# A state-space, mixture and attention block on one core: ScalarE applies the three normalisations, VectorE keeps their statistics

## The chip, the cores and the metric

One core of a Trainium2 chip runs the whole program. The metric is the device time of one execution in microseconds, as a median of several runs. PE is TensorE, DVE is VectorE, ACT is ScalarE, POOL is GpSimd and SP is SyncE, whose queue issues the transfers.

## The reference

The input is 4096 tokens of width 256 (two sequences of 2048). Four layers follow each other, each with a residual and a layer norm without scale behind it:

```
x = layernorm(x + mamba(x))      # the mamba normalises x once more at its start (with ln_g, ln_b)
x = layernorm(x + moe(x))        # 4 experts, two of them weighed per token
x = layernorm(x + attention(x))  # 16 heads, keys and values with a cross product
x = layernorm(x + ffn(x))
layernorm(x) = (x - mean) / sqrt(var + 1e-5)      # over the 256 features of a token
mamba: h[t] = exp(delta*A) * h[t-1] + delta*B*x,  y[t] = sum over 16 states of h[t]*C[t]
```

## The kernel before

The program has two stages with a barrier between them. The first, `mamba_moe_qkv`, holds everything up to the queries, keys and values; the second is the attention and the last layer. Only the first is changed.

The first stage cuts the tokens into 8 chunks of 512. A chunk lies in SBUF as `[128, 4, 256]` while tokens are on the partitions (`xn_tok`, `x1_tok`, `x2_tok`), and as `[128, 2 or 4, 512]` once it is transposed. Each engine runs the same function `iteration(i)` for i = -1 to 9 (i = 3 to 5 in a hardware loop). One iteration works on four chunks at once: `i` is scanned (16 states, one in each of 16 slots n), `f = i+1` is projected and convolved, `m = i-1` goes through the output projection, the router and the experts, and `q = i-2` gets its second norm and its queries, keys and values. The order on an engine is written out by hand through `if n == ...` lines; engines are tied by semaphores and each takes its instructions strictly in that order.

In one slot ScalarE forms four decays (`decays`, L708) for the slot after, VectorE multiplies (L952) and scans (L963) in two halves and copies the last column of `h` into `state`, times a flag that is 0 where a sequence begins (`keep_state`, L970). GpSimd then multiplies `h` by C (`times_c`, L1181) and adds it to `y` (`add_y`, L1192). The scan of a slot waits for the sum of two slots before it, since `h` has two buffers.

There are three norms of a chunk in this stage. For each, VectorE forms mean and variance of a token (`norm_stats`, L97 and L101) in the middle of a slot, GpSimd turns the variance into `r = (var + eps) ** -0.5` with two small operations (`scale`, L1249 and L1252), and VectorE applies the norm at the end of that slot with four tensor_scalar operations (`norm_apply`, L110), one for each 128 tokens:

```python
last = nc.vector.tensor_scalar(dst[:, i, :], src[:, i, :], mv[:, i, 0:1], r[:, i:i + 1],
                               ALU.subtract, ALU.mult)
```

- Norm 2, of chunk q, is applied in slot 1. `turn_x2` (PE, L572) transposes its result, behind `project_out` (L479) of chunk m; ScalarE copies it (L802), PE projects v (L563) and then z of chunk i (`project_z`, L449).
- Norm 1, of chunk m, is applied in slot 2. Its input needs `project_out` (the residual sum is L982). `turn_x1` (PE, L488) transposes its result in slot 3.
- Norm 0, of chunk i+2, is applied in slot 12 and transposed in slot 3 of the next iteration (`turn_xn`, L426).

ScalarE's order in slots 1 to 3 is: four decays, `y_begin` (L716); four decays, `copy_v` (L802, L805), `gates` (L722, the silu of z); four decays, `copy_qk` (L810 first: v by tokens, which frees a PSUM bank for the projection of q), `copy_x1` (L775), `copy_xn` (L728). In slot 4 it writes `xb` (L739), for which VectorE's `conv` (L912) waits. In slot 5 ScalarE's `routers` (L779) waits for VectorE's `crossed` (L1074, L1076), since both use `hid`. In slot 12 it copies B and C (`copy_bc`, L751), then four decays, then the copies of delta (L760).

Of the kernel before, what the change touches and what calls it, by code (L numbers as in the profile page):

```python
# [36 lines left out]
NORM_STEPS = 3  # L37
# [91 lines left out]
def mamba_moe_qkv(nc, a, scr, chunks=NCH):  # L129


    with ExitStack() as ctx:
# [28 lines left out]
        def col(name, i=0):  # L161
# [51 lines left out]
        powers = sb("powers", [P, 2, TT])  # L213
# [9 lines left out]
            q_stored k_stored kb_stored neg_ready powers_set ln0_scaled ln1_scaled ln2_scaled passed_sp passed_pe passed_dve passed_pool""".split()  # L223
# [71 lines left out]
        def _(sp):  # L295
# [31 lines left out]
            def store_x2(c):  # L327
                tok = bass.ds(c * CH, CH)
                sp.wait_ge(s["ln2_steps"], (c + 1) * NORM_STEPS)
                sp.dma_start(scr["x2"][tok, :].rearrange("(s p) n -> p s n", p=P), x2_tok[:])\  # L330
                    .then_inc(s["x2_stored"], 16)
# [77 lines left out]
        def _(pe):  # L409
# [10 lines left out]
            def turn_xn(c):  # L420
                pe.wait_ge(s["ln0_steps"], (c + 1) * NORM_STEPS)
# [61 lines left out]
            def turn_x1(c):  # L483
                pe.wait_ge(s["ln1_steps"], (c + 1) * NORM_STEPS)
# [82 lines left out]
            def turn_x2(c):  # L567
                pe.wait_ge(s["ln2_steps"], (c + 1) * NORM_STEPS)
# [131 lines left out]
        def _(act):  # L700
# [71 lines left out]

            def copy_x1(c):
# [58 lines left out]
            def iteration(i):  # L832
# [3 lines left out]
                for n in range(NS):  # L836
# [50 lines left out]
            act.wait_ge(s["setup_dve"], 5)  # L887
            iterations(act, iteration)
# [3 lines left out]
        def _(dve):  # L892
# [5 lines left out]

            def norm0_apply(c):
                dve.wait_ge(s["ln0_scaled"], 2 * c + 2)  # L900
                norm_apply(nc, s["ln0_steps"], xn_tok[:], xn_tok[:], ln_tmp)
# [76 lines left out]
            def norm1_stats(c):  # L978
                at_least(dve, s["ln2_steps"], c * NORM_STEPS)
# [7 lines left out]

            def norm1_apply(c):
                dve.wait_ge(s["ln1_scaled"], 2 * c + 2)
                norm_apply(nc, s["ln1_steps"], x1_tok[:], x1_tok[:], ln_tmp)  # L990
# [69 lines left out]

            def norm2_apply(c):
                dve.wait_ge(s["ln2_scaled"], 2 * c + 2)
                at_least(dve, s["x2_stored"], 16 * c)
                if not isinstance(c, int) or c > 0:
                    for k in range(KD):
                        wait_full(dve, c - 1, ("x2T", k))
                norm_apply(nc, s["ln2_steps"], x1_tok[:], x2_tok[:], ln_tmp)
# [32 lines left out]
            def iteration(i):  # L1100
# [3 lines left out]
                for n in range(NS):  # L1104
# [46 lines left out]
                    if n == 12 and inside(i + 2):  # L1151
                        norm0_apply(i + 2)
# [9 lines left out]
            v.memset(powers[:, 1], -0.5).then_inc(s["powers_set"], 1)  # L1162
            dve.wait_ge(s["w_mamba"], W_MAMBA)
# [6 lines left out]
            norm0_apply(0)  # L1170
# [4 lines left out]
        def _(pool):  # L1175
# [748 lines left out]
```

## Time and profile before

| | us |
|---|---|
| median of 3 runs (lowest, highest) | 4110.46 (4109.77, 4111.14) |
| the profiled execution, its own time | 4113.52 |
| its span, first to last instruction | 4111.7 |
| the first stage in it, up to the barrier | about 2172 |
| VectorE, TensorE, ScalarE, GpSimd busy over the span | 2964.8, 3500.6, 2195.3, 1515.1 |

Line numbers (L110) are lines of the kernel before. In a timeline row the first number is the start, the second the time from the start to the end of the group, and xN the number of instructions that were merged in it. In brackets stands the idle time of the engine ahead of the row and what ended it. A mean of a group is in ns.

### The profile page before, as it was taken

The page shows a single profiled execution, that of the slowest core. Times are in us where ns is not written, and L with a number is a line of the kernel's source. Part 1 is how long each engine was busy: PE and PEld are TensorE (multiplying, and loading weights), DVE is VectorE, ACT ScalarE, POOL GpSimd, SP SyncE. Part 2 cuts the span into 40 slices and gives each one's busy share as a digit, 9 for nine tenths or more (in the row PEclk, how much of TensorE's full clock was granted, in tenths as well). Part 3 has the DMA queues.
Part 4 walks back from the last instruction along what each step waited for, and adds up shares of the span by engine and source line. Part 5 has one row for each costly group of instructions (what it writes and reads, how often), then busy time and mean ns, then how long its engine had stood idle before and what let it go on. Part 6 is the DMA issues. An engine that isn't in the chain of part 4 may idle for free. (4 is left out here: it accounts for less than half of the span.)

```text
span 4111.7 us, 49896 instructions
## 1 busy us (share of the span) xinstructions
PE 3500.6 (85%) x14625; PEld 1599.7 (39%) x14625; DVE 2964.8 (72%) x3436; ACT 2195.3 (53%) x3556; POOL 1515.1 (37%) x1244
## 2 busy tenths in 40 slices
PE   4258888787878879788985999999999999999898
PEld 1025545354444545445540323222323232322565
DVE  4897786868778687685117878787878787878443
ACT  4344455545554454553210777777777777777221
POOL 2997686767777777687100000000000000000110
PEclk8579899899998989899995999999999999999999
DMA  2112112122121221212113000000000000000001
GB/s 95 31 37 65 61 53 77 54 70 78 57 75 44 80 69 60 70 59 98 49 36 99 17 18 17 18 21 21 18 18 17 18 17 18 22 20 29 15 31 36
DMA packets 110803, 183.45 MB, mean 45 GB/s; under 512 B 14495, under 2 KB 84599, under 8 KB 101817
## 3 DMA queue, kind: packets, MB, share of 16 engines
q1 hardware_dynamic: 110521, 180.09, 14.1%
q8 instruction: 128, 2.10, 0.2%
q14 instruction: 154, 1.26, 0.1%
HBM read 153.95 MB, written 26.09 MB: 44 GB/s over the span
## 5 line engine op out<-in xcount | busy, mean ns | idle before, releaser
L1688 DVE TENSOR_REDUCE tile_max<-ps 128x1 f32<-128x1024 f32 x1076 | 1268.1, 1220 | 287.5 <-PE ps L1479 284.9
L1633 ACT ACTIVATE probs<-ps 128x512 f32<-128x512 f32 x2056 | 1116.5, 598 | 492.4 <-PE ps L1493 467.2
L1181 POOL TENSOR_TENSOR h<-h,c_sb 128x512 f32<-128x512 f32 x512 | 678.7, 1356 | 421.9 <-DVE state L970 421.8
L1493 PE MATMUL ps<-qs,ks 101*128 101x512 bf16 x2056 | 712.8, 385 | 1.2
L1479 PE MATMUL ps<-ks,qs 99*128 99x512 bf16 x2152 | 668.8, 393 | 49.0 <-DMA ks<-scratch_kb 41.2
L963 DVE TENSOR_TENSOR_SCAN h<-decay,state,ps 128x512 f32<-128x512 f32 x512 | 627.5, 1267 | 58.5 <-POOL y_sum L1192 27.8
L1192 POOL TENSOR_TENSOR y_sum<-y_sum,h 128x512 f32<-128x512 f32 x512 | 641.3, 1284 | 8.5
L534 PE MATMUL ps<-x1T,e_w 128*128 128x512 f32 x1024 | 491.6, 629 | 103.0 <-ACT hid L779 102.6
L1503 PE MATMUL ps<-probs,vh 128*32 128x512 f32 x4096 | 551.5, 611 | 24.5 <-issue 24.5
L1805 POOL COPY vh<-v_all 128x256 f32 (+1 forms) x32 | 12.7, 402 | 1433.4 <-PE ps L1503 1368.1
L555 PE MATMUL ps<-e_w,hid 128*128 128x256 f32 x2048 | 454.2, 380 | 11.2 <-ACT hid L779 7.5
L1493 PEld LDWEIGHTS ps<-qs,ks 101*128 101x128 bf16 x2056 | 198.9, 97 | 644.2 <-ACT probs L1633 434.9
L779 ACT ACTIVATE hid<-ps,cols 128x512 f32<-128x512 f32 x288 | 193.2, 686 | 452.2 <-PE ps L534 423.7
L555 PEld LDWEIGHTS ps<-e_w,hid 128*128 128x128 f32 x2048 | 386.7, 190 | 82.2 <-issue 28.4
L708 ACT ACTIVATE decay<-delta,neg_a 128x512 f32<-128x512 f32 x512 | 335.0, 712 | 136.1 <-DVE h L963 129.7
L534 PEld LDWEIGHTS ps<-x1T,e_w 128*128 128x128 f32 x1024 | 202.4, 202 | 365.0 <-issue 225.7
L952 DVE TENSOR_TENSOR ps<-du,ps 128x1024 f32<-128x1024 f32 x256 | 312.5, 1221 | 6.5 <-PE ps L417 3.3
L1479 PEld LDWEIGHTS ps<-ks,qs 99*128 99x128 bf16 x2152 | 208.8, 99 | 274.3 <-issue 50.5
L1052 DVE SCALAR_TENSOR_TENSOR x_tok<-ps,cw,x_tok 128x256 f32<-128x256 f32 x128 | 55.2, 473 | 270.4 <-PE ps L555 270.4
L417 PE MATMUL ps<-bc,sel 96*128 96x512 bf16 x128 | 53.8, 421 | 169.6 <-DVE ps L952 169.6
L1503 PEld LDWEIGHTS ps<-probs,vh 128*32 128x32 f32 x4096 | 81.0, 108 | 220.6 <-ACT probs L1633 179.4
L479 PE MATMUL ps<-w_out,gate 128*128 128x256 f32 x256 | 76.7, 473 | 67.0 <-DVE x_tok L1052 62.7
(172 smaller groups left out, 3002.6 us busy)
## 6 DMA issues: line engine op xcount, KB each, us to landing
e_w<-in_e_w SPq DMA_DIRECT2D x64, 1024.0 KB, 7.0
c_sb<-scratch_c SPq DMA_DIRECT2D x128, 256.0 KB, 3.5
qs<-scratch_q SPq DMA_DIRECT2D x210, 64.0 KB
ks<-scratch_k SPq DMA_DIRECT2D x210, 64.0 KB
scratch_q<-parts SPq DMA_DIRECT2D x16, 384.0 KB, 4.0
scratch_k<-parts SPq DMA_DIRECT2D x16, 384.0 KB, 7.5
xr<-scratch_x SPq DMA_DIRECT2D x10, 512.0 KB, 4.0
xn_tok<-in_x SPq DMA_DIRECT2D x8, 512.0 KB, 4.9
```

Source lines behind the costliest of these rows:

```text
L534: last = mm(bank(key), e_w1[:, e % 2, k, i * P:(i + 1) * P], x1T[:, k, :], start=k == 0, stop=k == KD - 1)
L555: last = mm(ps[:, DOWN_BANK[at], i * D:(i + 1) * D], hid[:, k, (2 * pair + i) * P:(2 * pair + i + 1) * P], e_w2[:, e % 2, k, :], start=k = ...
L708: fn(decay[:, n % 2, m, :], delta[:, m, :], ACT.Exp, scale=neg_a[:, n * DB + m:n * DB + m + 1]).then_inc(s["decay_ready"], 1)
L952: v.tensor_tensor(ps[:, 0:2, :], du[:, 2 * half:2 * half + 2], ps[:, 2 + n % 2:3 + n % 2, :].to_broadcast([P, 2, CH]), ALU.mult)\
L963: v.tensor_tensor_scan(h[:, n % 2, m, :], decay[:, n % 2, m, :], ps[:, m % 2, :], state[:, n, m:m + 1], ALU.mult, ALU.add)\
L1181: last = nc.gpsimd.tensor_tensor(h[:, n % 2, m, :], h[:, n % 2, m, :], c_sb[:, n % C_RING, :], ALU.mult)
L1192: last = nc.gpsimd.tensor_tensor(y[:, m, :], y[:, m, :], h[:, n % 2, m, :], ALU.add)
L1479: last = mm(ps[:, slot(side) + i, :], qs[0:K_MAX, j, t * P:(t + 1) * P], ks[0:K_MAX, j, k * CH:(k + 1) * CH], start=True, stop=True)
L1493: mm(ps[:, S_BANK[i], :], ks[0:K_ALL, j, step * P:(step + 1) * P], qs[0:K_ALL, j, qc * CH:(qc + 1) * CH], start=True, stop=True).then_inc( ...
L1503: last = mm(ps[qc * VW:(qc + 1) * VW, AV_BANK, :], vh[:, j, step, :], probs[:, step % 2, qc, :], start=step == 0, stop=step == KT - 1)
L1633: fn(probs[:, step % 2, qc, :], ps[:, S_BANK[i], :], ACT.Exp)\
L1688: v.tensor_reduce(tile_max[:, t, half:half + 1], ps[:, slot(side):slot(side) + PAIR, :].rearrange("p a n -> p (a n)"), AX.X, ALU.max).then ...
```

## The change

ScalarE applies the norm with its own scale and bias, `x * r + (-mean * r)`. GpSimd forms the bias with two more small operations (four in all for each norm). VectorE keeps the statistics. Those who waited for the third step of the statistics semaphore (`turn_xn`, `turn_x1`, `turn_x2`, `store_x2`, `norm1_stats`) wait for a semaphore that ScalarE raises. Norm 2 stands on ScalarE in slot 1 behind `y_begin`, norm 1 in slot 2 behind `gates`, norm 0 in slot 12 behind `copy_bc`. Apart from this, `keep_state` takes the flag as a scalar operand of tensor_scalar where it was a second tensor.

```diff
-def norm_apply(nc, steps, src, dst, tmp):
-    mv, r = tmp[1], tmp[5]
+def norm_apply(nc, done, src, dst, tmp):
+    r, shift = tmp[5], tmp[6]
     for i in range(src.shape[1]):
-        last = nc.vector.tensor_scalar(dst[:, i, :], src[:, i, :], mv[:, i, 0:1], r[:, i:i + 1],
-                                       ALU.subtract, ALU.mult)
-    last.then_inc(steps, 1)
+        last = nc.scalar.activation(dst[:, i, :], src[:, i, :], ACT.Identity, scale=r[:, i:i + 1],
+                                    bias=shift[:, i:i + 1])
+    last.then_inc(done, 1)
...
+            def norm0(c):
+                act.wait_ge(s["ln0_scaled"], (c + 1) * SCALE_STEPS)
+                norm_apply(nc, s["ln0_done"], xn_tok[:], xn_tok[:], ln_tmp)
+            def norm1(c):
+                act.wait_ge(s["ln1_scaled"], (c + 1) * SCALE_STEPS)
+                norm_apply(nc, s["ln1_done"], x1_tok[:], x1_tok[:], ln_tmp)
+            def norm2(c):
+                act.wait_ge(s["ln2_scaled"], (c + 1) * SCALE_STEPS)
+                at_least(act, s["x2_stored"], 16 * c)
+                if not isinstance(c, int) or c > 0:
+                    for k in range(KD):
+                        wait_full(act, c - 1, ("x2T", k))
+                norm_apply(nc, s["ln2_done"], x1_tok[:], x2_tok[:], ln_tmp)
...
                     if n == 1 and inside(i):
                         y_begin(i)
+                    if n == 1 and inside(q):
+                        norm2(q)
                     if n == 2:
                         if inside(q):
                             copy_v(q)
                         if inside(i):
                             gates(i)
+                        if inside(m):
+                            norm1(m)
...
                     if n == 12 and inside(f):
                         copy_bc(f)
+                    if n == 12 and inside(i + 2):
+                        norm0(i + 2)
...
-                v.tensor_tensor(state[:, n, :], h[:, n % 2, :, CH - 1], keep.to_broadcast([P, DB]), ALU.mult)\
+                v.tensor_scalar(state[:, n, :], h[:, n % 2, :, CH - 1], keep, None, ALU.mult)\
...
-                    if n == 1 and inside(q):
-                        norm2_apply(q)
-                    if n == 2 and inside(m):
-                        norm1_apply(m)
-                    if n == 12 and inside(i + 2):
-                        norm0_apply(i + 2)
...
-                pool.wait_ge(s[name + "_steps"], c * NORM_STEPS + 2)
-                nc.gpsimd.tensor_tensor(ln_tmp[2], ln_tmp[1][:, :, 1], powers[:, 0], ALU.add)\
-                    .then_inc(s[name + "_scaled"], 1)
-                pool.wait_ge(s[name + "_scaled"], c * 2 + 1)
-                nc.gpsimd.tensor_tensor(ln_tmp[5], ln_tmp[2], powers[:, 1], ALU.pow)\
-                    .then_inc(s[name + "_scaled"], 1)
+                pool.wait_ge(s[name + "_steps"], (c + 1) * NORM_STEPS)
+                nc.gpsimd.tensor_tensor(ve, mv[:, :, 1], powers[:, 0], ALU.add).then_inc(scaled, 1)
+                nc.gpsimd.tensor_tensor(half, mv[:, :, 0], powers[:, 2], ALU.mult).then_inc(scaled, 1)
+                pool.wait_ge(scaled, at + 1)
+                nc.gpsimd.tensor_tensor(r, ve, powers[:, 1], ALU.pow).then_inc(scaled, 1)
+                pool.wait_ge(scaled, at + 3)
+                nc.gpsimd.tensor_tensor(shift, half, r, ALU.mult).then_inc(scaled, 1)
```

## Rows read from the trace of the kernel before

**Rows 1.** Window: length, busy of PE, PEld, DVE, ACT, POOL; clock; DMA share; GB/s

```profile
1100.00:1350.00 250.00, 205.03 (x641) 117.36 (x640) 192.16 (x217) 126.71 (x175) 184.42 (x151) 0.91 0.21 66
```

**Rows 2.** VectorE's groups of lines in the first stage: busy, mean | idle before

```profile
L970 DVE TENSOR_TENSOR state<-h,cols 128x4 f32<-128x4 f32 x128 | 60.9, 476 | 4.8 <-DVE h L963 0.2
L110 DVE TENSOR_SCALAR x_tok<-x_tok,ln_mv,ln_r 128x256 f32<-128x256 f32 x64 | 60.0, 997 | 4.8 <-POOL ln_r L1252 4.2 <-issue 0.5
...
L110 DVE TENSOR_SCALAR xn_tok<-xn_tok,ln_mv,ln_r 128x256 f32<-128x256 f32 x32 | 29.3, 976 | 2.9 <-POOL ln_r L1252 2.9
...
L1085 DVE TENSOR_SCALAR k_f<-k_f,temp 128x512 f32<-128x512 f32 x16 | 7.0, 479 | 0.0
```

**Rows 3.** VectorE's timeline in iteration 5 (1211 to 1465 us)

```profile
1240.59 4.99 DVE L110 TENSOR_SCALAR x_tok<-x_tok,ln_mv,ln_r 128x256 f32<-128x256 f32 x4 [0.19 <-issue]
...
1281.01 0.75 DVE L912 SCALAR_TENSOR_TENSOR xb<-ps,cols,xb 128x509 f32<-128x509 f32 x1 [3.06 <-ACT xb L739]
...
1289.38 2.94 DVE L1074 TENSOR_TENSOR soft<-soft,hid 48x512 f32<-48x512 f32 x2
```

**Rows 4.** TensorE's timeline in the same iteration, slots 1 to 3

```profile
1234.62 9.01 PE L479 MATMUL ps<-w_out,gate 128*128 128x256 f32 x32 [8.83 <-DVE x_tok L1052]
...
1245.64 1.09 PE L572 MATMUL ps<-ident,x_tok 128*128 128x128 f32 x8 [1.79 <-DVE x_tok L110]
...
1251.01 7.03 PE L449 MATMUL ps<-xnT,w_in 128*128 128x512 f32 x16
...
1263.08 10.10 PE L563 MATMUL ps<-x1T,wqkv 128*128 128x512 f32 x16 [3.95 <-ACT hid L810]
```

**Rows 5.** ScalarE's timeline in the same iteration

```profile
1258.69 1.28 ACT L708 ACT_TABLE_LOAD   x1
1259.98 2.56 ACT L708 ACTIVATE decay<-delta,neg_a 128x512 f32<-128x512 f32 x4
1262.45 1.06 ACT L810 ACTIVATE hid<-ps 128x512 f32<-128x512 f32 x2
...
1432.16 0.69 ACT L760 ACTIVATE pre<-ps,cols 128x512 f32<-128x512 f32 x1 [7.59 <-PE ps L466]
```

**Rows 6.** Who waited for VectorE's L110, and for L1076

```profile
  PE ps L572: 12.8, 7
...
  ACT hid L779: 3.8, 3
...
  ACT L779: 3.7, 3
```

**Rows 7.** ScalarE's groups of lines in the first stage

```profile
L708 ACT ACTIVATE decay<-delta,neg_a 128x512 f32<-128x512 f32 x512 | 335.0, 712 | 136.1 <-DVE h L963 129.7 <-DVE delta L937 5.5
L739 ACT ACTIVATE xb<-ps,cols 128x512 f32<-128x512 f32 x32 | 24.7, 772 | 0.0
...
L738 ACT ACTIVATE halo<-ps 128x3 f32<-128x3 f32 x32 | 5.5, 173 | 89.7 <-PE ps L437 89.7
```

**Rows 8.** GpSimd's timeline in iteration 5: slot 1 and slot 4

```profile
1252.38 0.20 POOL L1249 TENSOR_TENSOR ln_ve<-ln_mv,powers 128x4 f32<-128x4 f32 x1 [4.43 <-DVE ln_mv L101]
...
1290.29 1.50 POOL L1235 CAST parts<-q_f 128x1024 bf16<-128x1024 f32 x1
```

**Rows 9.** Tail, GpSimd idle: norm 2 of chunk 7, and the routers of chunk 7

```profile
2123.77 1.38 DVE L110 TENSOR_SCALAR x_tok<-x_tok,ln_mv,ln_r 128x256 f32<-128x256 f32 x4 [1.40 <-POOL ln_r L1252]
...
2125.21 1.97 PE L572 MATMUL ps<-ident,x_tok 128*128 128x128 f32 x8 [5.73 <-DVE x_tok L110]
...
1985.26 0.69 ACT L779 ACTIVATE hid<-ps,cols 128x512 f32<-128x512 f32 x1 [2.20 <-DVE soft L1076]
```

**Rows 10.** VectorE's timeline in iteration 0: norm 0 is applied

```profile
206.73 5.25 DVE L110 TENSOR_SCALAR xn_tok<-xn_tok,ln_mv,ln_r 128x256 f32<-128x256 f32 x4
```

**Rows 11.** Windows with the granted clock (third from the end) in iteration 5

```profile
1262.00:1263.00 1.00, 0.00 (x0) 0.00 (x0) 1.00 (x1) 1.00 (x3) 1.00 (x2) 0.63 0.00 0
...
1269.00:1270.00 1.00, 1.00 (x3) 0.38 (x2) 0.17 (x1) 0.21 (x1) 1.00 (x2) 0.95 0.47 164
```

More of the change, by code:

```diff
@@ L36 @@
 LN_STEPS = 16
-NORM_STEPS = 3
+NORM_STEPS = 2
+SCALE_STEPS = 4
 RSQRT_SEED = 0x5F3759DF
@@ L212, in mamba_moe_qkv @@
         ln_tmp = ln_buffers(sb, "ln")
-        powers = sb("powers", [P, 2, TT])
+        powers = sb("powers", [P, 3, TT])
         ps = ctx.enter_context(nc.psum_tensor("ps1", [P, 8, CH], F32))
@@ L222, in mamba_moe_qkv @@
             parts_steps x2_stored v_stored
-            q_stored k_stored kb_stored neg_ready powers_set ln0_scaled ln1_scaled ln2_scaled passed_sp passed_pe passed_dve passed_pool""".split()
+            q_stored k_stored kb_stored neg_ready powers_set ln0_scaled ln1_scaled ln2_scaled ln0_done ln1_done ln2_done passed_sp passed_pe passed_dve passed_pool""".split()
         s = {n: sem(n) for n in names}
@@ L328, in store_x2 @@
                 tok = bass.ds(c * CH, CH)
-                sp.wait_ge(s["ln2_steps"], (c + 1) * NORM_STEPS)
+                sp.wait_ge(s["ln2_done"], c + 1)
                 sp.dma_start(scr["x2"][tok, :].rearrange("(s p) n -> p s n", p=P), x2_tok[:])\
@@ L420, in turn_xn @@
             def turn_xn(c):
-                pe.wait_ge(s["ln0_steps"], (c + 1) * NORM_STEPS)
+                pe.wait_ge(s["ln0_done"], c + 1)
                 at_least(pe, s["gate_ready"], c * DB)
@@ L483, in turn_x1 @@
             def turn_x1(c):
-                pe.wait_ge(s["ln1_steps"], (c + 1) * NORM_STEPS)
+                pe.wait_ge(s["ln1_done"], c + 1)
                 pe.wait_ge(s["gate_ready"], upto(c + 2) * DB)
@@ L567, in turn_x2 @@
             def turn_x2(c):
-                pe.wait_ge(s["ln2_steps"], (c + 1) * NORM_STEPS)
+                pe.wait_ge(s["ln2_done"], c + 1)
                 for k in range(KD):
@@ L887, in _ @@
             act.wait_ge(s["setup_dve"], 5)
+            norm0(0)
             iterations(act, iteration)
@@ L897, in norm0_stats @@
                 norm_stats(nc, dve, s["ln0_steps"], c, xn_tok[:], ln_tmp, s["passed_dve"])
-            def norm0_apply(c):
-                dve.wait_ge(s["ln0_scaled"], 2 * c + 2)
-                norm_apply(nc, s["ln0_steps"], xn_tok[:], xn_tok[:], ln_tmp)
             def conv(c, pair):
@@ L978, in norm1_stats @@
             def norm1_stats(c):
-                at_least(dve, s["ln2_steps"], c * NORM_STEPS)
+                at_least(dve, s["ln2_done"], c)
                 dve.wait_ge(s["out_mm"], c + 1)
@@ L986, in norm1_stats @@
                 norm_stats(nc, dve, s["ln1_steps"], c, x1_tok[:], ln_tmp, s["passed_dve"])
-            def norm1_apply(c):
-                dve.wait_ge(s["ln1_scaled"], 2 * c + 2)
-                norm_apply(nc, s["ln1_steps"], x1_tok[:], x1_tok[:], ln_tmp)
             def logits(c):
@@ L1059, in norm2_stats @@
                 norm_stats(nc, dve, s["ln2_steps"], c, x1_tok[:], ln_tmp, s["passed_dve"])
[L1061 to L1067, printed above, removed]
             def crossed(c):
@@ L1162, in _ @@
             v.memset(powers[:, 1], -0.5).then_inc(s["powers_set"], 1)
+            v.memset(powers[:, 2], -1.0).then_inc(s["powers_set"], 1)
             dve.wait_ge(s["w_mamba"], W_MAMBA)
@@ L1169, in _ @@
             norm0_stats(0)
-            norm0_apply(0)
             iterations(dve, iteration)
@@ L1246, in scale @@
             def scale(name, c):
-                pool.wait_ge(s[name + "_steps"], c * NORM_STEPS + 2)
-                nc.gpsimd.tensor_tensor(ln_tmp[2], ln_tmp[1][:, :, 1], powers[:, 0], ALU.add)\
-                    .then_inc(s[name + "_scaled"], 1)
-                pool.wait_ge(s[name + "_scaled"], c * 2 + 1)
-                nc.gpsimd.tensor_tensor(ln_tmp[5], ln_tmp[2], powers[:, 1], ALU.pow)\
-                    .then_inc(s[name + "_scaled"], 1)
+                stats, mv, ve, half, seed, r, shift = ln_tmp
+                scaled, at = s[name + "_scaled"], c * SCALE_STEPS
+                pool.wait_ge(s[name + "_steps"], (c + 1) * NORM_STEPS)
[5 more added lines that the diff above has]
+                nc.gpsimd.tensor_tensor(shift, half, r, ALU.mult).then_inc(scaled, 1)
             def iteration(i):
@@ L1275, in iteration @@
                         split(q, 1, k_f[:], n - 9)
-            pool.wait_ge(s["powers_set"], 2)
+            pool.wait_ge(s["powers_set"], 3)
             scale("ln0", 0)
```

## The prediction

> **What bounds the kernel now.** I read the windows first, then VectorE's groups of lines, then the timelines of one steady iteration engine by engine, following each wait to what ended it. In the windows VectorE is the busiest engine of the first stage beside TensorE, 192 and 205 of 250 us [rows 1], so relief for VectorE looks valuable. The 96 tensor_scalar of the three norms took 60.0 + 29.3 = 89.3 us and 7.7 us of idle time ahead of them [rows 2]. This is the most that the move could bring if VectorE were the path everywhere.
>
> The timelines say that it mostly is not. Behind norms 2 and 1 VectorE runs into slot 4 and stands idle for 3.06 us for ScalarE's `xb` [rows 3]. That wait ends a chain that does not touch VectorE from slot 1 on: `project_out`, `turn_x2` (TensorE idle for 1.79 us until norm 2 is applied), the v and z projections, the gates, a table load, four decays, the copy of v (L810), and only then the projection of q, ahead of which TensorE idles for 3.95 us [rows 4, 5]. So in slots 1 to 4 the path is TensorE and ScalarE in turn, and ScalarE is without a pause from the last gate to L810. In the later slots TensorE and ScalarE drive each other as well. Norm 0 in slot 12 is followed on ScalarE by a pause of 7.59 us for TensorE [rows 5].
>
> A mean of 997 and 976 ns [rows 2] for a tensor_scalar that takes 1.38 us for four when GpSimd is idle [rows 9] shows that they queue behind GpSimd: with GpSimd at work four took 4.99 and 5.25 us [rows 3, 10].
>
> **The change, part by part.** All of it is summed against the profiled execution's 4113.5 us (span 4111.7 and 1.8 around it), which lies 3.1 above the median.
>
> *Price of a norm on ScalarE.* No row has this form. A 512-wide ACTIVATE from SBUF with one pointer operand takes 712 ns; from PSUM, one with two takes 772 and one with one (L760) 690, so the second pointer costs about 85: 797 ns. Four decays took 2.56 us, so each further one adds 0.62 and 0.10 is overlap; a column costs, by the step from three columns (173 ns) to 512 (L810, about 590), 0.82 ns. For 256 columns that makes 0.587 for the first and 0.49 for each further: 2.05 us for the four. The bounds are half of the 2.56 (1.3) and four without overlap (2.35). I take 2.05. A table load is not added: L739 has the same function and no load of its own [rows 5, 7].
>
> The Trainium skill, ScalarE: Activation LUTs, Rules for kernel authors, tells the author to use VectorE and not ScalarE for add and mul. Here its advice holds only against an idle GpSimd (1.38 against about 2.05 us); where GpSimd was busy the four took 5.0 and 5.2 us on VectorE. By the rule each move costs 0.7 us and the 24 norms would add 16 us if all were on the path; the sum below goes by place instead.
>
> *GpSimd's two further operations.* They are of the form that takes 0.20 us [rows 8]; with the step between dependent ones about 0.5 us more until the bias is ready. It matters where nothing else is waited for.
>
> *Norm 2, iterations 2 to 7.* Its scale and bias are ready about 2 us after the statistics, near 1238.4 in iteration 5; applied by 1240.5. TensorE needs it at 1243.9, behind `project_out` and a broadcast, so 3.3 us of slack. The wait for L110 goes: TensorE's 12.8 us in all less the 5.7 of the last chunk [rows 6, 9] is −7.1. ScalarE's decays for slot 3 end at 1243 and VectorE wants them at about 1248.
>
> *Norm 1.* It stands between the last gate and the table load, where ScalarE had no pause [rows 5], so L810 and everything behind comes 2.05 later: six iterations, +12.3. In iteration 1 the same place lies ahead of `copy_x1` with no norm 2 to give anything back: +2.1. What VectorE saves in slots 1 and 2 (about 8 us) becomes idle time ahead of `conv`.
>
> *`crossed`, slot 5.* Its first two operations took 2.94 us in iteration 5, since GpSimd was in its copy of q until 1291.8 [rows 3, 8]. GpSimd's run from slot 1 to there is without a gap and begins when norm 1's variance is there; it was idle 4.43 us before that [rows 8], of which VectorE's earlier arrival gives back about 2.5. So the copy ends before `crossed` starts. ScalarE waited 3.8 + 3.7 us for L1076, 2.2 of it in the tail, where GpSimd was idle [rows 6, 9]: −5.3.
>
> *Norm 0.* From iteration 1 it is hidden on both engines by the 7.59 us [rows 5]; without that cover it would be 2.05 for each chunk. In iteration 0, where VectorE is the path to the end, 5.25 us [rows 10] leave it. But the sums of GpSimd then bound the scan of slot 13 (the timeline puts GpSimd only 0.5 behind), and operations behind it queue again: of 5.25 some 1.8 remain: −1.8. The very first norm is on the path: 0.5 + 0.67 = +1.1.
>
> *Tail.* Norm 1 of chunk 7 delays L810 by +1.3; norm 2 of chunk 7, alone on the path, costs 0.5 + 0.7 = +1.2 [rows 9].
>
> *The clock.* TensorE's pause ahead of q grows from 3.95 to about 6 us. In the row before, its granted clock fell to 0.5 (1.2 GHz) at the end of the pause and was back at 2.4 GHz in the window at 1269; the 16 matmuls took 10.10 where 16 alike took 7.03 [rows 4, 11]. A longer pause can put part of the low stretch into the pause (−1 each) or bring a second one (+1.7 each). I take +0.3 each: +2.
>
> *The kept state.* 128 of 476 ns, 60.9 us in all [rows 2]. A form that does not queue behind GpSimd would take about 0.2. But a wide tensor_scalar from SBUF to SBUF takes 479 ns for 512 columns, thus two columns a cycle, and L110, a tensor_scalar too, queues [rows 2]. So I expect it to queue as before, and where it does not queue, to be 0 to 0.05 us longer. Most of the queued ones lie where VectorE waits anyway. From −6 (all queueing gone, on the few slots of iterations 0 and 1 where VectorE is the path) to +1; I take 0.
>
> The Trainium skill, SBUF — State Buffer on-chip working memory, SBUF: two separate sides, says that VectorE and GpSimd share one pair of ports under an exclusive lock, needed by an operation in a two-port mode or with two SBUF inputs. By it the scalar operand removes one reason for the lock and a two-port mode keeps another, so the edit gives nothing; the sum would not change by it.
>
> Sum: −7.1 + 12.3 + 2.1 − 5.3 − 1.8 + 1.1 + 2.5 + 2 = +5.8. 4113.5 + 5.8 = 4119.3 for a profiled execution, and 4116 for the median. The second stage is untouched.
>
> **The rivals.**
> - *Forecast (0.50):* the sum. With 1.3 to 2.35 for a norm (−5 to +2) and the clock's bounds (−8 to +8), its own range is 4106 to 4127.
> - *The kept state leaves the queue (0.15).* For it: its four elements need no fast mode. Against: L110. −6 on the sum: 4110, no change.
> - *The longer pause costs the clock (0.17), slower.* Place: ahead of the projection of q and, in iteration 1, ahead of `turn_xn`. Price: a second low stretch costs 1.7 us more, 7 times: +12, 4128 or so. It decides once the pause exceeds the 3.95 us after which the clock now falls just as work resumes. Against it: part of the stretch may lie in the pause.
> - *ScalarE's queue is the bound everywhere (0.07), slower.* Norms 2 and 0 would be on the path too, 2 × 2.05 × 6 = +25: 4141. For norm 2 it needs GpSimd's bias 3.3 us later than I have it, for norm 0 the 7.59 us used up.
> - *VectorE's queue is the path after all (0.11), faster.* Then the 97 us less what GpSimd and ScalarE add: with two thirds of it 4050, with the part that I find idle wrong by a quarter, 4090. Against: the idle 3.06 us at `conv`.
>
> **How the numbers follow.** A measurement here tells 0.2% (8.2 us) from no change. The forecast's case lies above 4118.7 in about 3 of 10: same 0.34, slower 0.15, faster 0.01. With the others: same 0.34 + 0.12 + 0.01 = 0.47; slower 0.15 + 0.16 + 0.07 = 0.38; faster 0.01 + 0.03 + 0.11 = 0.15. The predicted time is 4116. The range 4100 to 4134 leaves out the faster case, ScalarE's queue and little more.
>
> **What would show it.** Right: no wait of `turn_x2` for the norm in iterations 2 to 7; L810 about 2 us later behind the gates; four ACTIVATEs in 2.0 to 2.1 us; VectorE's idle time ahead of L912 in slot 4 grown by about 8 us; ScalarE's wait for L1076 near 0 in those iterations; no further table loads; L970 queueing as before. Wrong: table loads ahead of the norms, L970 near 200 ns throughout, an idle VectorE nowhere in slot 4, or the 16 matmuls of q and k above 11 us.

## The result: 0.38% slower

| | before | after |
|---|---|---|
| median of 6 runs each, us (lowest, highest) | 4110.22 (4107.52, 4111.14) | 4124.82 (4121.84, 4131.06) |
| profiled execution, own time; span | 4113.52; 4111.7 | 4126.50; 4124.7 |
| mean granted clock of TensorE in it | 0.922 | 0.917 |
| start of VectorE's work in the second stage in it | 2174.5 | 2187.0 |

The ratio of after to before is 1.0038 (95% interval 1.0025 to 1.0051): slower, and by more than the 0.2% that a measurement here can't tell from no change. The forecast was 4116 with a range of 4100 to 4134, and the range holds the result; its likeliest case, "no change" (0.47, against 0.38 for slower), did not come. The loss is all in the first stage: +12.5 of +13.0 us of the span.

The page of the kernel after says that the work did move (busy time of the engines; x is the number of instructions). VectorE has 81 us less than before, ScalarE 45 us more, and TensorE, with the same 14625 matmuls, 10.6 us more:

```profile
PE 3511.2 (85%) x14625; PEld 1606.1 (39%) x14625; DVE 2883.9 (70%) x3341; ACT 2240.3 (54%) x3652; POOL 1514.2 (37%) x1292
```

The groups of lines of the first stage after, ScalarE's and VectorE's. The norms take 588 and 589 ns each and come without table loads of their own (ScalarE has 171 table loads in the whole program, before and after). The kept state, 476 ns in [rows 2], is now 620. The idle time ahead of `conv` stands in the last column of its row, 85.6 us; before (L912) it was 55.1:

```profile
L709 ACT ACT_TABLE_LOAD x73 | 93.7, 1283 | 27.6 <-issue 16.4 <-DVE delta L957 10.0
L111 ACT ACTIVATE x_tok<-x_tok,ln_t,ln_r 128x256 f32<-128x256 f32 x64 | 33.1, 589 | 77.1 <-POOL ln_t L1258 77.1
L111 ACT ACTIVATE xn_tok<-xn_tok,ln_t,ln_r 128x256 f32<-128x256 f32 x32 | 16.5, 588 | 9.6 <-POOL ln_t L1258 9.6
```
```profile
L990 DVE TENSOR_SCALAR state<-h,cols 128x4 f32<-128x4 f32 x128 | 79.3, 620 | 4.9 <-DVE h L983 0.5
L932 DVE SCALAR_TENSOR_TENSOR xb<-ps,cols,xb 128x509 f32<-128x509 f32 x32 | 23.6, 744 | 85.6 <-ACT xb L740 85.6
```

Iteration 5 after (1222 to 1471 us), TensorE's timeline, to be held against [rows 4]. `turn_x2` (L573) now waits for nothing, and the pause ahead of the projection of q (L564) is 5.90 us where it was 3.95. Behind it the 16 matmuls took 8.82 us, less than the 10.10 of before; that holds for this iteration and not for most of the others, as the table further down shows:

```profile
1246.01 9.77 PE L480 MATMUL ps<-w_out,gate 128*128 128x256 f32 x32 [8.84 <-DVE x_tok L1068]
...
1255.84 1.04 PE L573 MATMUL ps<-ident,x_tok 128*128 128x128 f32 x8
1257.61 3.70 PE L564 MATMUL ps<-x1T,wqkv 128*128 128x512 f32 x8 [0.74 <-ACT x1T L819]
1261.15 7.03 PE L450 MATMUL ps<-xnT,w_in 128*128 128x512 f32 x16
...
1275.18 8.82 PE L564 MATMUL ps<-x1T,wqkv 128*128 128x512 f32 x16 [5.90 <-ACT hid L827]
```

ScalarE's timeline of the same stretch, against [rows 5]. Norm 2 is applied by 1251.99, 3.85 us before TensorE comes to `turn_x2`. Norm 1 (1268.71) lies in a run without a pause, from the last gate to L827:

```profile
1249.91 2.08 ACT L111 ACTIVATE x_tok<-x_tok,ln_t,ln_r 128x256 f32<-128x256 f32 x4 [5.67 <-POOL ln_t L1258]
...
1268.22 0.60 ACT L723 ACTIVATE gate<-ps 128x512 f32<-128x512 f32 x1 [1.12 <-PE ps L450]
1268.71 2.06 ACT L111 ACTIVATE x_tok<-x_tok,ln_t,ln_r 128x256 f32<-128x256 f32 x4
1270.79 1.28 ACT L709 ACT_TABLE_LOAD   x1
1272.09 2.56 ACT L709 ACTIVATE decay<-delta,neg_a 128x512 f32<-128x512 f32 x4
1274.55 1.05 ACT L827 ACTIVATE hid<-ps 128x512 f32<-128x512 f32 x2
```

VectorE, against [rows 3]: 7.37 us idle where it was 3.06, and `crossed` (its two operations took 2.94) no longer queues:

```profile
1293.24 0.75 DVE L932 SCALAR_TENSOR_TENSOR xb<-ps,cols,xb 128x509 f32<-128x509 f32 x1 [7.37 <-ACT xb L740]
...
1301.90 1.26 DVE L1082 TENSOR_TENSOR soft<-soft,hid 48x512 f32<-48x512 f32 x2
```

Who waited for whom over the whole run after (us in all, times, longest), against [rows 6]. TensorE waits for a norm ahead of `turn_x2` once, in the tail, and ScalarE for `crossed` 2.9 us where it was 3.8 + 3.7:

```profile
PE ps L573 <- ACT x_tok L111: 6.7, 1, 6.7
...
ACT hid L796 <- DVE soft L1084: 2.9, 2, 2.5
```

So nearly every mechanism that was forecast is there. What takes the 13 us? A window over each of the iterations 2 to 6, from the start of VectorE's `delta` to the next, gives it; columns as in [rows 1]. Before, then after:

```profile
472.03:715.79 243.76, 200.97 (x644) 115.27 (x643) 188.75 (x217) 126.75 (x176) 184.15 (x150) 0.94 0.22 68
715.79:964.64 248.85, 205.20 (x643) 116.68 (x643) 191.34 (x216) 126.79 (x176) 184.55 (x151) 0.92 0.22 66
964.64:1210.81 246.17, 201.57 (x644) 115.48 (x643) 191.93 (x217) 126.84 (x176) 183.89 (x150) 0.93 0.21 67
1210.81:1465.23 254.42, 209.45 (x644) 119.00 (x643) 193.73 (x217) 126.71 (x176) 183.60 (x150) 0.90 0.21 65
1465.23:1714.27 249.04, 205.59 (x644) 117.84 (x643) 185.28 (x204) 126.89 (x176) 181.67 (x147) 0.92 0.20 64
```
```profile
471.21:723.88 252.67, 207.99 (x644) 119.12 (x643) 178.91 (x205) 132.29 (x188) 181.75 (x155) 0.91 0.21 65
723.88:971.15 247.27, 204.29 (x643) 117.72 (x643) 177.70 (x204) 132.46 (x188) 184.05 (x157) 0.92 0.20 67
971.15:1222.28 251.13, 207.49 (x644) 118.93 (x643) 179.49 (x205) 132.38 (x188) 183.13 (x156) 0.90 0.21 65
1222.28:1471.29 249.01, 205.34 (x644) 118.00 (x643) 178.26 (x204) 132.49 (x188) 183.38 (x156) 0.91 0.22 66
1471.29:1723.96 252.67, 208.29 (x644) 119.26 (x643) 177.28 (x196) 130.36 (x184) 181.34 (x151) 0.91 0.20 63
```

Read the first two numbers behind the times together. TensorE executes the same 644 matmuls in each row, so its busy time says how many of them ran at the lower of its two clocks (1.2 and 2.4 GHz; the mean granted clock stands third from the end). The length less this busy time is all the waiting. Summed over the five rows:

| iterations 2 to 6, us | length | TensorE busy | length less busy |
|---|---|---|---|
| before | 1242.24 | 1022.78 | 219.46 |
| after | 1252.75 | 1033.40 | 219.35 |

The waiting is equal to 0.1 us. The +10.5 us are matmuls at the low clock: TensorE was busy at 1.2 GHz for 117.5 us of these five iterations before and for 141.7 after, and its busy time less half of that, thus as it would be at 2.4 GHz throughout, is 964.0 and 962.6 us.

The extra time has several places. The up projections of the experts (L534 before) took 6.1 us more in the five iterations, the router's second one (L504) 5.3, and the projections of v, q and k (L563) 3.1; other lines took 3.9 less. Of all pauses only the one ahead of q grew by more than 0.1 us an iteration. The 16 matmuls behind it, us:

| iteration | 2 | 3 | 4 | 5 | 6 | sum |
|---|---|---|---|---|---|---|
| before, pause 3.94 to 3.95 | 8.83 | 8.77 | 8.61 | 10.10 | 8.81 | 45.12 |
| after, pause 5.90 to 5.91 | 10.10 | 9.01 | 10.15 | 8.82 | 10.17 | 48.25 |

Most of the rest came behind pauses that had not grown. Behind the same pause of 6.50 us in iteration 2 the same eight matmuls took 5.14 us before and 6.57 after. TensorE's timelines, before and after:

```profile
655.18 5.14 PE L534 MATMUL ps<-x1T,e_w 128*128 128x512 f32 x8 [6.50 <-ACT hid L779]
```
```profile
661.81 6.57 PE L535 MATMUL ps<-x1T,e_w 128*128 128x512 f32 x8 [6.50 <-ACT hid L796]
```

### The profile page after: what moved, and what is told of

It is laid out like the page before. It is cut to its first block and busy times, and to the rows that moved or that the text cites. A ratio compares the mean times of both kernels' runs of the same rounds, so it can differ in the third digit from the quotient of the medians.

```text
span 4124.7 us, 49939 instructions
## 1 busy us (share of the span) xinstructions
PE 3511.2 (85%) x14625; PEld 1606.1 (39%) x14625; DVE 2883.9 (70%) x3341; ACT 2240.3 (54%) x3652; POOL 1514.2 (37%) x1292
## 5 line engine op out<-in xcount | busy, mean ns | idle before, releaser
L535 PE MATMUL ps<-x1T,e_w 128*128 128x512 f32 x1024 | 500.0, 638 | 102.2 <-ACT hid L796 101.7
L564 PE MATMUL ps<-x1T,wqkv 128*128 128x512 f32 x192 | 106.0, 711 | 43.3 <-ACT hid L827 37.0
```

The lines of the kernel that those rows point to most:

```text
L535: last = mm(bank(key), e_w1[:, e % 2, k, i * P:(i + 1) * P], x1T[:, k, :], start=k == 0, stop=k == KD - 1)
```

## The experiments

Each ratio is to runs of the kernel before on the same chip in the same job.

### One part alone, and norm 1 at another place

Theory: norm 1 costs its 2.05 us in each iteration by standing ahead of L827, and the clock adds to it. The rivals were the kept state, and ScalarE's work as such.

**Kept state alone**, on the kernel before:

```diff
-                v.tensor_tensor(state[:, n, :], h[:, n % 2, :, CH - 1], keep.to_broadcast([P, DB]), ALU.mult)\
+                v.tensor_scalar(state[:, n, :], h[:, n % 2, :, CH - 1], keep, None, ALU.mult)\
```

> The kernel before with one edit: the kept state takes its factor as a scalar operand (one tensor_scalar, as in the kernel after); the norms stay on VectorE. In the kernel after the 128 kept-state operations took 620 ns in the mean (shortest 228) where before it was 476 ns (shortest 161), so the form does not leave the queue behind GpSimd. Theory (the scalar operand costs 0.07 us wherever the operation does not queue, and queues at least as often): mean about 0.53 to 0.62 us here, and the kernel 0 to 3 us slower than before, thus no measurable difference. Rival (the edit alone is worth something: the longer mean in the kernel after comes from GpSimd being at other work when VectorE arrives earlier): mean at or below 0.476 us, and the kernel up to 6 us faster. A second rival (the edit carries the loss): 4120 or more.

Measured: 4120.52 (9 runs, 4112.19 to 4130.05) against 4110.05, ratio 1.0030 (1.0018 to 1.0043). The group of VectorE took 550 ns where it was 476:

```profile
L970 DVE TENSOR_SCALAR state<-h,cols 128x4 f32<-128x4 f32 x128 | 70.3, 550 | 4.9 <-DVE h L963 0.5
```

The operation costs what was expected, 9.4 us of VectorE's time in all, mostly where VectorE waits anyway. The kernel's time does not follow: the forecast of at most 3 us failed and the second rival's number (4120 or more) came out. Its runs show why that rival is not the whole answer. The profiled one took 4112.8, at a mean granted clock of 0.922; the runs at 0.922 took 4112.2 and 4112.8, those at 0.918 and 0.919 4125.2 to 4130.1. The kernel before took 4110.0 to 4114.8 at 0.922 in the same job, and 4122.1 to 4123.4 at 0.919 in a later one. So at one clock the medians differ by 1.3 us (at 0.922) and 4.4 us (at 0.919, across two jobs), and the rest came with a lower clock in more of the runs. The profiled run itself has iterations 2 to 6 of 1238.97 us, 3.3 less than before, with 1018.04 of TensorE busy.

**The norms alone**: the kernel after, with the kept state as before (the same diff backwards, on L990).

> The kernel after with the kept state multiplied as before (tensor_tensor with a broadcast factor); the three norms stay on ScalarE. Theory (the loss of 14.6 us in the median is norm 1 in ScalarE's gapless run plus what TensorE's clock costs behind it): within 3 us of the kernel after, about 4122 to 4125. Rival (the kept state's scalar operand carries the loss): back to 4110 to 4113.

Measured: 4121.47 (4117.61 to 4125.90), ratio 1.0033 (1.0021 to 1.0045): close to the theory's 4122 to 4125, and far from the rival's 4110 to 4113. Both parts are slower alone by 0.30 and 0.33% and together by 0.38%, so the losses don't add, and can't be read as two prices of two edits.

**Norm 1 later on ScalarE**: behind the two copies of v by tokens, ahead of the copies of q.

```diff
-                        if inside(m):
-                            norm1(m)
                     if n == 3:
+                        if inside(q):
+                            copy_vtok(q)          # the first loop of copy_qk
+                        if inside(m):
+                            norm1(m)
                         if inside(q):
                             copy_qk(q)            # the rest of it
```

> The kernel after with norm 1 moved on ScalarE from behind the gates (slot 2) to behind the two copies of v by tokens (slot 3), ahead of the copies of q, where ScalarE stood idle for about 3.4 us before. Theory (norm 1 costs its 2.05 us because it lies between the last gate and the copy of v on which the projection of q waits): TensorE's pause ahead of q falls from 5.90 back to about 3.95 us, seven iterations give back 2.05 us each less what norm 1 now delays turn_x1 by, so 10 to 14 us, and the clock's part with it: 4097 to 4112. With the other savings kept it should end at or below the kernel before. Rival 1 (ScalarE's total work is what counts, not the place): within 3 us of the kernel after. Rival 2 (turn_x1 and the router now wait for norm 1, and the loss only moves): the pause ahead of q is gone and one of about 2 us stands ahead of turn_x1, 4120 to 4128.

Measured: 4127.61 (4113.95 to 4132.12), ratio 1.0037 (1.0023 to 1.0051). The mechanism of the theory is in the trace, its total (4097 to 4112) is not. The numbers of both rivals came out: within 3 us of the kernel after, and 4120 to 4128. But the pause of about 2 us ahead of `turn_x1` that the second one asks for is not there (the transposes follow the projection without a wait in iterations 2 to 7), and the first, that the place does not count, does not fit the pause: ahead of q it is 3.94 us again, and norm 1 is applied while TensorE projects q. TensorE's timeline in iteration 5, then ScalarE's:

```profile
1282.24 9.79 PE L564 MATMUL ps<-x1T,wqkv 128*128 128x512 f32 x16 [3.94 <-ACT hid L827]
```
```profile
1281.62 1.05 ACT L827 ACTIVATE hid<-ps 128x512 f32<-128x512 f32 x2
1282.57 2.06 ACT L111 ACTIVATE x_tok<-x_tok,ln_t,ln_r 128x256 f32<-128x256 f32 x4
```

**Norm 1 on VectorE**, at the end of slot 2 as before; norms 0 and 2 on ScalarE.

```diff
+            def norm1_apply(c):
+                dve.wait_ge(s["ln1_scaled"], (c + 1) * SCALE_STEPS)
...
+                for i in range(TT):
+                    last = v.tensor_scalar(x1_tok[:, i, :], x1_tok[:, i, :], mv[:, i, 0:1], r[:, i:i + 1],
+                                           ALU.subtract, ALU.mult)
+                last.then_inc(s["ln1_done"], 1)
...
+                    if n == 2 and inside(m):
+                        norm1_apply(m)
```

> The kernel after with norm 1 applied by VectorE at the end of slot 2 as before; norms 0 and 2 stay on ScalarE. Theory (only norm 1 lies on the path on ScalarE; norm 2 gives back 7 us of waits of TensorE and the early start of GpSimd's run 5 us): 14 us of the mechanical sum go away, the pause ahead of q is about 3.95 us again, and the kernel runs at 4098 to 4108. GpSimd's run still starts a little earlier than before. Rival (norms 2 and 0 on ScalarE cost as much as norm 1): 4118 or more. Rival (VectorE, now longer by about 5 us in slot 2, is late for conv in slot 4 and gives nothing back): 4108 to 4114.

Measured: 4117.85 (11 runs, 4106.75 to 4124.78), ratio 1.0014 (1.0003 to 1.0026), against a forecast of 4098 to 4108 and a rival (norms 2 and 0 cost as much as norm 1) at 4118 or more. Its iterations 2 to 6:

```profile
466.74:719.30 252.56, 209.87 (x643) 119.81 (x643) 182.18 (x208) 130.36 (x184) 182.14 (x155) 0.90 0.20 65
719.30:972.26 252.96, 211.63 (x643) 120.62 (x643) 182.39 (x208) 130.32 (x184) 184.49 (x157) 0.89 0.20 65
972.26:1221.50 249.24, 207.55 (x644) 117.90 (x643) 182.62 (x208) 130.35 (x184) 183.50 (x156) 0.90 0.21 66
1221.50:1470.67 249.17, 207.50 (x644) 117.89 (x643) 182.69 (x209) 130.34 (x184) 183.47 (x156) 0.90 0.21 66
1470.67:1722.83 252.16, 210.02 (x644) 119.87 (x643) 179.60 (x200) 128.41 (x180) 181.41 (x151) 0.90 0.20 63
```

The same sums for all, from such windows:

| iterations 2 to 6, us | length | TensorE busy | length less busy |
|---|---|---|---|
| before | 1242.24 | 1022.78 | 219.46 |
| after | 1252.75 | 1033.40 | 219.35 |
| kept state alone | 1238.97 | 1018.04 | 220.93 |
| norms alone | 1252.75 | 1034.30 | 218.45 |
| norm 1 late | 1255.91 | 1046.42 | 209.49 |
| norm 1 on VectorE | 1256.09 | 1046.57 | 209.52 |

Each row is one execution. The first two columns go with that execution's clock: the profiled run of the kept state alone was nearly the fastest of nine, that of norm 1 late the slowest of seven (4132.12). The last column depends on that much less: within norm 1 on VectorE it stayed at 41.3 to 42.7 us an iteration while TensorE's busy time went from 207.5 to 211.6. It shows both halves of the theory's mechanics, so the rivals' numbers came out without their mechanisms. Either way of taking norm 1 out of ScalarE's gapless run removes 9.8 us of waiting from five iterations, 1.97 each, against 2.05 forecast. And these two kernels wait 9.9 us less than the kernel before; norm 2 and `crossed` were forecast at 7.1 and 5.3 over six iterations, so at 10.3 over five. The middle column takes it away again: TensorE is busy for 13 us more than after and 24 more than before, 21 of these 24 on the up projections of the experts (L534). That made the clock the question. Within one kernel the time goes with it too: norm 1 on VectorE took 4106.8 to 4110.8 us at a mean clock of 0.920 and 4117.9 to 4124.8 at 0.916 and 0.917.

### TensorE's pauses filled

If the low stretches come from TensorE's pauses, matmuls in the pauses should keep the clock up. They multiply weights by weights into a PSUM bank that nobody holds there, and nothing reads them:

```diff
+            def fill(b, n):
+                for k in range(n):
+                    mm(ps[:, b, :], w_in[:, 0, 0:P], w_in[:, 0, 0:CH], start=True, stop=True)
...
                     if n == 0 and inside(q):
                         down(q, NE - 1, 1)
+                        if inside(i):
+                            wait_free(pe, q, ("x2T", 0))
+                            fill(6 + use[("x2T", 0)] % 2, 14)
                     if n == 1 and inside(m):
+                        if inside(q) and inside(i):
+                            fill(6 + use[("x2T", 0)] % 2, 16)
                         project_out(m)
```

Three more stand ahead of the projection of q (`fill(4, 8)`, behind a wait for the gates) and in the middle of the ups of slots 9 and 11 (`fill(4, 6)`, `fill(5, 12)`).

> The kernel before, with matmuls added that compute nothing used (constant weights against constant weights, into a bank of PSUM that is free there) in four pauses of TensorE of each iteration that has all chunks inside: 14 behind the last down of slot 0, 16 ahead of project_out, 8 ahead of the projection of q, 6 and 12 within the ups of slots 9 and 11. So many fit in the pauses at 0.44 us each. In the runs so far the time follows the mean granted clock: over 61 executions of six kernels, each 0.001 of the mean clock goes with 3.8 us, and at one clock (0.922) the kernels would stand at 4112.6 before, 4108.9 after, 4113.7 kept state alone, 4106.4 norms alone, 4103.1 norm 1 late, 4099.5 norm 1 on VectorE. Theory (every pause of TensorE can bring a low stretch, and the length and place of the pauses decide how many; this is worth more than the edits): with the pauses filled the clock stays up behind them, and the kernel is 30 to 80 us faster than before, 4030 to 4080. Rival 1 (the low stretches are not caused by the pauses): no change or slower by what the added matmuls delay. Rival 2 (added work makes the throttle act more): lower mean clock, slower than 4120.

> The kernel after with the same added matmuls (12 ahead of the projection of q, as its pause is 5.9 us). Theory (the change saves some us of work and waits, and loses them by the clock): with the clock held up, this kernel is 0 to 8 us faster than the kernel before with the same fill, and at least level with it. Rival (the change costs by ScalarE's 2.05 us and not by the clock): it stays 10 to 15 us slower than the kernel before with the same fill.

> The kernel after with norm 1 on VectorE, with the same added matmuls (8 ahead of the projection of q). At one clock it stood 13 us below the kernel before. Theory: 8 to 16 us below the kernel before with the same fill, and the fastest of the four. Rival (the clock-corrected figure is an artefact of fitting): level with the filled kernel before within 5 us.

> The kernel before with the kept state's scalar operand alone, and the same added matmuls. Alone it was 10 us slower in the median with a mean clock of 0.920, yet at one clock only 1 us slower. Theory (its loss is the clock's, by where its small shifts put the pauses): within 3 us of the filled kernel before. Rival (the operand itself costs 10 us by its longer queueing): 8 to 12 us slower than the filled kernel before.

| the first filled kernels | median (range), us | ratio to before (95%) | mean clock, profiled run |
|---|---|---|---|
| before | 4189.54 (4181.35 to 4196.89) | 1.0200 (1.0186, 1.0215) | 0.947 |
| after | 4224.03 (4219.52 to 4234.30) | 1.0285 (1.0270, 1.0299) | 0.945 |
| norm 1 on VectorE | 4187.39 (4185.23 to 4193.48) | 1.0195 (1.0181, 1.0209) | 0.947 |
| kept state alone | 4184.74 (4181.25 to 4186.37) | 1.0184 (1.0170, 1.0198) | 0.948 |

None came out as forecast. The filled kernel before, forecast at 4030 to 4080, took 4190; the filled kernel after was 34 us above that one, where theory (0 to 8 below) and rival (10 to 15 above) both failed; norm 1 on VectorE was 2 us below it and not 8 to 16, as its rival had it; the kept state was 5 us below, not within 3. Each call is two matmuls in the trace, and the fill was twice as long as the pauses. The second one of the filled kernel before, TensorE's timeline, with `project_out` right behind it:

```profile
1260.97 13.90 PE L422 MATMUL ps<-w_in 128*128 128x512 f32 x32
1274.70 5.56 PE L483 MATMUL ps<-w_out,gate 128*128 128x256 f32 x25
```

It took the place of an idle time of 8.83 us [rows 4]. As timings of the change they are useless (after has four more calls ahead of q, 3.5 us in each iteration). Two things hold. First, the clock went up from 0.922 to 0.947, so rival 2 falls; and in iterations 2 to 6 the kernel's own matmuls took 976.3 us of TensorE's time (its busy time less the fill) instead of 1022.8, so the low stretches do go with the pauses, and rival 1 falls too. Second, the kept state alone, 0.30% slower before, is not slower than its filled partner (4184.7 against 4189.5), so the operand does not cost 10 us by itself.

Then with calls that fit: 7, 9, 4 (6 for the kernel after), 3 and 7.

> The kernel before with about half of the added matmuls of the first filled kernels: one call of 512 columns is two matmuls in the trace, 0.87 us, and not one of 0.44, so the earlier counts were twice too long for their pauses (12.2 and 13.9 us where 7.2 and 8.8 were free) and delayed the path by some 20 us an iteration, while the clock did stay up (6.8 us of TensorE's busy time at 1.2 GHz in iteration 5 against 33.5). Now 7, 9, 4, 3 and 7 calls: 6.1, 7.8, 3.5, 2.6 and 6.1 us. Theory (the low stretches follow TensorE's pauses, and half of TensorE's busy time in them is lost): iterations 2 to 6 take about 239 to 242 us instead of 243.7 to 254.4, the kernel is 40 to 60 us faster than before, 4050 to 4075. Rival (the clock matters little for the end, since ScalarE and VectorE set it): within 10 us of 4110.

> The kernel after with the fitted fill (7, 9, 6, 3 and 7 calls; the pause ahead of the projection of q is 5.9 us here). In the traces, the lengths of iterations 2 to 6 less half of TensorE's busy time at 1.2 GHz are 235.7, 236.3, 237.4, 237.7, 236.3 us before and 237.2, 235.5, 236.1, 236.2, 237.0 after: 1.4 us less in all after. Theory (the change's work is about level or up to 4 us better, and its loss is the clock's): within 6 us of the filled kernel before, more likely below it. Rival (ScalarE's 2.05 us of norm 1 is the loss): 10 to 15 us above the filled kernel before.

> The kernel after with norm 1 on VectorE and the fitted fill (7, 9, 4, 3 and 7 calls). Its iterations 2 to 6 less half of TensorE's busy time at 1.2 GHz were 235.2, 233.7, 234.2, 234.2, 234.7 us: 11.4 us less than the kernel before in all. Theory: 8 to 16 us below the filled kernel before, and the fastest of all, 4040 to 4065. Rival (the difference was only another place of the low stretches): level with the filled kernel before within 4 us.

> The kernel after with norm 1 on ScalarE behind the two copies of v by tokens, and the fitted fill (7, 9, 4, 3 and 7 calls). At one clock this order stood 9.5 us below the kernel before and 3.6 above norm 1 on VectorE. Theory (on ScalarE norm 1 costs only by its place in front of the copies of v): 20 us or so below the kernel after with the fitted fill (4091), and within 5 us of norm 1 on VectorE with the fitted fill (4069). Rival (norm 1 on ScalarE costs its 2.05 us an iteration anywhere): 4080 to 4090.

| fitted fill | median (range), us | ratio to before (95%) | profiled run: time, clock | its iterations 2 to 6 |
|---|---|---|---|---|
| before | 4110.16 (4105.91 to 4114.60) | 0.9988 (0.9979, 0.9998) | 4105.91, 0.941 | 1239.65 |
| after | 4091.43 (4085.51 to 4099.66) | 0.9940 (0.9925, 0.9955) | 4092.26, 0.945 | 1211.63 |
| norm 1 on VectorE | 4069.08 (4067.49 to 4072.63) | 0.9887 (0.9871, 0.9904) | 4069.46, 0.947 | 1216.26 |
| norm 1 late | 4090.85 (4082.70 to 4101.03) | 0.9968 (0.9956, 0.9980) | 4082.70, 0.943 | 1209.59 |

TensorE's time on the kernel's own matmuls in iterations 2 to 6, and all the rest (waiting and fill), us:

| | own matmuls | waiting and fill |
|---|---|---|
| before, as it was | 1022.8 | 219.5 |
| before, fitted fill | 1003.3 | 236.3 |
| after, as it was | 1033.4 | 219.4 |
| after, fitted fill | 979.9 | 231.8 |

With its pauses filled the kernel after is faster than the kernel before with its pauses filled, by 18.7 us in medians of one job. It has two more calls ahead of q; but the two kernels with norm 1 elsewhere, with four calls there as in the kernel before, are faster than that kernel as well. The sign of the change turns when the pauses are filled, as the theory had it; the size was forecast too small, and the clock is not level between the two (0.945 against 0.941). The kernel before gained only 4 us of the 40 to 60 forecast: its own matmuls took 19.5 us less, and waiting and fill 16.9 more, 11.4 of it one wait, which TensorE's timeline shows. With a full clock `project_out` takes 7.17 us instead of 9.01 [rows 4], and TensorE then waits 3.61 us for norm 2, where it was 1.79:

```profile
1230.37 7.17 PE L483 MATMUL ps<-w_out,gate 128*128 128x256 f32 x32 [1.33 <-DVE x_tok L1072]
...
1241.37 1.97 PE L583 MATMUL ps<-ident,x_tok 128*128 128x128 f32 x8 [3.61 <-DVE x_tok L110]
```

VectorE began the norm 5.98 us behind the start of `project_out` (5.97 before), and its four operations queued behind GpSimd as before:

```profile
1236.35 4.97 DVE L110 TENSOR_SCALAR x_tok<-x_tok,ln_mv,ln_r 128x256 f32<-128x256 f32 x4 [0.19 <-issue]
```

The eight transposes behind this new pause took 1.97 us where the kernel after, also filled, needs 1.04 and waits for nothing:

```profile
1215.40 7.17 PE L484 MATMUL ps<-w_out,gate 128*128 128x256 f32 x32 [1.34 <-DVE x_tok L1088]
1222.41 0.38 PE L418 MATMUL ps<-bc,sel 96*128 96x512 bf16 x1
1222.63 1.04 PE L584 MATMUL ps<-ident,x_tok 128*128 128x128 f32 x8
```

So the new pause costs twice, as a wait and by the clock behind it, and norm 2 on ScalarE removes both: in iterations 2 to 6 of the kernel after, also filled, the wait is 17.9 us shorter, the transposes take 4.8 less and the projections of v, q and k 10.4 less. This is the change's gain, and it is larger the faster TensorE is. In the profiled run of the kernel after the second stage, which has neither fill nor change, took 1952.4 us against 1938.0 in the filled kernel before, so the first stage alone is 28.1 us shorter there. Of the 14.4 us, 9.0 are TensorE's busy time, at a mean granted clock of 0.955 against 0.961; why is open.

Norm 1 on VectorE with the fitted fill is the fastest kernel of the study, 1.13% faster than the kernel before. Its lead over the filled kernel before, 41 us, is more than the 8 to 16 forecast, while its time lies above the 4040 to 4065 that was forecast. Norm 1 late, forecast within 5 us of it, is 22 us slower in the median (by the ratios, each to its own job, 0.8%), and the theory's number failed; its rival, that norm 1 on ScalarE costs its 2.05 us anywhere, had 4080 to 4090, next to the measured one. In its profiled run, the fastest of its seven, iterations 2 to 6 are nevertheless the shortest of all (1209.59), so norm 1 costs nothing there. It lost in iteration 1 (232.3 us against 220.0) and in iteration 7 (462.9 against 455.4), which have less of the fill, and where TensorE was busy 9.3 and 5.2 us longer for the same work (189.18 against 179.89, 402.92 against 397.75).

## Why the prediction came out as it did

- *Price of a norm on ScalarE, no table loads*: right. Four took 2.06 to 2.08 us (forecast 2.05).
- *GpSimd's bias, +0.5 us, and norm 2 applied in time, −7.1*: right; `turn_x2` waits only in the tail. The rule of the Trainium skill, ScalarE: Activation LUTs, Rules for kernel authors (add and mul belong on VectorE), does not hold at this place: in the filled kernel before, norm 2 took 4.97 us on VectorE and TensorE waited for it, against 2.08 on ScalarE in iteration 5 of the kernel after.
- *Norm 1 ahead of L810, +2.05 in each iteration*: right. Undone in two ways it gave 1.97 each. In iteration 1, +2.1 forecast, the iteration was 2.1 us shorter instead; TensorE's busy time was 3.55 less there, so its waiting grew by 1.4.
- *`crossed` no longer queues, −5.3*: right in iteration 5 (1.26 for 2.94 us, as VectorE's timeline has it); ScalarE's wait fell from 7.5 to 2.9 us, −4.6.
- *Norm 0*: iteration 0 was 1.4 us shorter (1.8 forecast). The first norm and what lies behind it cost 2.7 up to the first `delta`, not 1.1.
- *Tail, +2.5*: from the start of iteration 7 to the end of the stage it was 2.85 us longer, but 2.75 of it is TensorE's busy time. The waiting grew by 0.1 us, so the term is not borne out.
- *VectorE's saving becomes idle time ahead of `conv`, about 8 us*: right in kind, about half in size. It grew from 3.06 to 7.37 us in iteration 5, and from 3.1 to 7.6 in the mean of iterations 2 to 6.
- *Kept state, 0*: no better than that. Its mean rose from 476 to 620 ns (550 on the kernel before), so it still queues, as the row for L110 had let expect. That agrees with the Trainium skill, SBUF — State Buffer, SBUF: two separate sides, by which a VectorE operation in a two-port mode has to wait while a GpSimd operation holds the ports that the two share. Waiting of iterations 2 to 6 was 0.9 us more with it than without (219.35 against 218.45), and 1.5 more on the kernel before. The rival that it leaves the queue is excluded.
- *The sum without the clock*, +3.8: measured 13.0 less the 10.6 of TensorE's busy time, +2.4.
- *The clock, +0.3 each, +2 in all*: this is the term that was mis-sized. It measured +10.6, thus 8.6 more than the +2, just beyond the 8 that the forecast allowed it. I looked for it only where a pause grew, ahead of the projection of q. There the 16 matmuls took 3.1 us more in iterations 2 to 6, in three iterations slower by 1.3 to 1.5 us and in iteration 5 faster by 1.3. Most of the rest came behind pauses that had not grown. That the total lies inside the range although this term and the tail were off is luck in part.
- *The rival "the longer pause costs the clock"* had the right sign and, by luck, the right size (4128): only about a third of the extra time (3.1 of 10.6 us) lies at its place. *ScalarE's queue everywhere* is excluded by norm 2's slack and by the late norm 1. *VectorE's queue is the path*: no, with the clock as it was; its 7.37 us idle ahead of `conv` say so.

Shown: the mechanics of each move, that the loss is matmuls at the low clock, and that filling the pauses raises the clock and turns the sign of the change. Not shown: why the change led to more of them, and what decides how long the clock stays low behind a given pause. The same pause and the same work gave 5.14 and 6.57 us, and the runs of one kernel spread by up to 18 us, largely with its clock. Why the kernels with the least waiting got the most low clock, and why the kept state alone fell on a low clock in more runs, is left open.

## What to carry to other kernels

Before pricing a move of a few microseconds, split an iteration into TensorE's busy time and the rest: where the same matmuls take several per cent more or less time from iteration to iteration, an edit that shifts everything can land elsewhere in that spread, and this can be larger than the edit's own price. Judge the edit by the rest, and treat the pauses themselves as the cost: here closing them with matmuls that are thrown away made a version at least 1.1% faster than either kernel, and turned a change of +0.4% into one of −0.5%. An operation that another engine takes over belongs where that engine waits, and a norm that queues behind GpSimd is cheap only as long as TensorE is slow enough not to notice.

## What the runs showed of the hardware

Work that computes nothing can make a program faster: with 400 further matmuls in the trace (of 14625) the kernel with norm 1 on VectorE ran at a mean granted clock of 0.947 instead of 0.916 in its profiled run, and in 4069 instead of 4118 us in the median. A tensor_scalar with a pointer operand on four elements a partition took 0.23 us on VectorE when GpSimd was idle and up to 2.07 beside a busy GpSimd; the tensor_tensor with two SBUF inputs before it took 0.16 and up to 2.15. The time of one kernel varied by 6 to 18 us in a job of 7 to 22 runs, and mostly with its mean clock: norm 1 on VectorE took 4107 to 4111 us at 0.920 and 4118 to 4125 at 0.916 and 0.917.
